# Experts of a mixture: the downs of two pairs in one run, the gate chain between the steps of the ups, the router in two row halves

## What is computed

```python
logits = flat @ router_w.T                        # flat: 512 x 64, layer-normed; 8 experts
probs = softmax(logits)
topk_probs, topk_idx = top_k(probs, 2)
topk_probs = topk_probs / (sum(topk_probs) + 1e-09)
gates = einsum('nk,nke->ne', topk_probs, onehot(topk_idx))
h1 = einsum('nc,ehc->neh', flat, w1)              # 682 hidden per expert
h3 = einsum('nc,ehc->neh', flat, w3)
y = einsum('neh,ech->nec', silu(h1) * h3, w2)
out = einsum('ne,nec->nc', gates, y)              # all experts are computed, the gate picks
```

## Time and profile before

| | us |
|---|---|
| median of three timed runs | 197.92 |
| lowest, highest | 196.71, 240.08 |
| profiled execution, its own time | 196.59 |
| span of the profiled execution | 194.8 |
| busy in it: TensorE, VectorE, ScalarE, GpSimd | 186.6, 151.4, 134.6, 97.9 |

### The profile page before, as it was taken

One profiled execution on the slowest core, in us unless ns is written; L12 is line 12 of the kernel. 1 busy time (PEld: TensorE's weight loads), 2 busy tenths in 40 slices (PEclk: granted clock), 3 DMA queues, 4 the chain that ended last, 5 costly groups with the idle time before them and its releaser, 6 DMA issues.

```text
span 194.8 us, 2708 instructions
## 1 busy us (share of the span) xinstructions
PE 186.6 (96%) x764; PEld 88.1 (45%) x766; DVE 151.4 (78%) x253; ACT 134.6 (69%) x298; POOL 97.9 (50%) x100
## 2 busy tenths in 40 slices
PE   7899999899999998999999999989999999999994
PEld 2334644354546453555455256836333324333332
DVE  6586899989999999999999955657776724888503
ACT  3729897999999999999999515355755614666200
POOL 6516667798999999999999700000000133100000
PEclk9999999999999999999999999799999999999999
DMA  5699372477768996799777993000000442000000
GB/s 155 140 227 191 112 257 106 179 219 255 235 214 240 294 308 220 251 309 303 244 265 214 192 204 47 3 0 0 2 3 3 128 114 59 24 0 3 0 0 27
DMA packets 23452, 28.00 MB, mean 144 GB/s; under 512 B 8153, under 2 KB 12734, under 8 KB 23438
## 3 DMA queue, kind: packets, MB, share of 16 engines
q1 hardware_dynamic: 23118, 27.67, 49.6%
q10 hardware_dynamic: 320, 0.16, 0.3%
HBM read 27.38 MB, written 0.44 MB: 143 GB/s over the span
## 4 chain that ended last, share of the span: by engine, by line
PE 67%; POOL 13%; issue 6%; DMA 5%; DVE 4%; ACT 3%; SPq 2%; POOLq 0%; DVEq 0%
PE ps L1246 17%; PE ps L1020 16%; POOL rings L474 12%; PE ps L1266 10%; PE ps L1027 4%; DMA cr<-bc_rows 3%; PE ps L1131 2%; DMA w_conv<-conv_w_dram 2%; PE ps L1006 2%; PE ps L985 1%; PE ps L945 1%; PE ps L1002 1%; ACT si L643 1%; PE ps L1046 1%; PE ps L1204 1%
## 5 line engine op out<-in xcount | busy, mean ns | idle before, releaser
L474 POOL TENSOR_TENSOR rings<-rings,cr 128x512 f32<-128x512 f32 x59 | 73.4, 1281 | 6.6 <-DVE rings L758 5.0
L758 DVE TENSOR_TENSOR_SCAN rings<-rings,ps 128x512 f32<-128x512 f32 x64 | 73.7, 1201 | 0.6
L566 ACT ACTIVATE rings<-delta,a_neg 128x510 f32<-128x510 f32 x64 | 46.7, 782 | 0.7 <-DVE rings L758 0.6
L643 ACT ACTIVATE si<-ps 128x512 f32<-128x512 f32 (+1 forms) x44 | 26.3, 597 | 23.0 <-PE ps L1246 23.0
L1246 PE MATMUL ps<-fd,wup 64*128 64x512 f32 (+1 forms) x136 | 40.3, 600 | 0.8 <-DVE fd L860 0.5
L547 ACT ACTIVATE scaled<-ps,b_tok 128x128 f32<-128x128 f32 x124 | 37.2, 443 | 0.0
L1020 PE MATMUL ps<-rings,ident 128*128 128x512 f32 x64 | 32.4, 599 | 1.0 <-POOL rings L474 0.9
L1020 PE MATMUL ps<-rings,flip 128*128 128x512 f32 x64 | 31.9, 601 | 0.5 <-POOL rings L474 0.2
L918 DVE TENSOR_TENSOR rings<-ps,si 128x512 f32<-128x512 f32 (+1 forms) x31 | 21.2, 690 | 13.5 <-ACT si L643 13.1
L496 POOL TENSOR_TENSOR fdg<-fd,gb 64x512 f32<-64x512 f32 x4 | 5.0, 1274 | 50.1 <-DMA gb<-g_rows 50.1
L1246 PEld LDWEIGHTS ps<-fd,wup 64*128 64x128 f32 (+1 forms) x136 | 15.7, 182 | 22.9 <-DVE rings L918 12.2
(11 more groups left out here) (222 smaller groups left out, 193.1 us busy)
## 6 DMA issues: line engine op xcount, KB each, us to landing
cr<-bc_rows SPq DMA_DIRECT2D x48, 256.0 KB, 4.0
br<-bc_rows SPq DMA_DIRECT2D x17, 256.0 KB, 4.4
cr<-c_rows SPq DMA_DIRECT2D x12, 256.0 KB, 3.7
wup<-w_up_dram SPq DMA_DIRECT2D x8, 341.0 KB, 6.3
wdn<-w_down_dram SPq DMA_DIRECT2D x4, 160.0 KB
wdn<-w_down_dram SPq DMA_DIRECT2D x4, 128.0 KB
gb<-g_rows SPq DMA_DIRECT2D x4, 128.0 KB, 4.6
delta<-g_rows SPq DMA_DIRECT2D x4, 128.0 KB, 3.6
```

Of the source, the lines that this page charges most:

```text
L474: nc.gpsimd.tensor_tensor(hc[:, q], hs[:, q], cr[:, row_slot(n)] if n >= ROWS_FROM else cs[:, q], ALU.mult).then_inc(weighted, 1)
L566: nc.scalar.activation(da[:, q, :, 1:L], delta[:, k, :].rearrange("p (b l) -> p b l", b=B)[:, :, 1:L], ACT.Exp, scale=a_neg[:, k * N + col ...
L643: nc.scalar.activation(si[0:rows, S % 2, :], ps[0:rows, BANK_H + 2 * (S % 3), :], ACT.Silu).then_inc(silu_ready, 1)
L758: nc.vector.tensor_tensor_scan(hs[:, q, :], da[:, q].rearrange("p b l -> p (b l)"), driven(q), 0.0, ALU.mult, ALU.add).then_inc(scanned, 1)
```

## The change

1. Downs in two runs: the downs of pairs 0 and 1 come together behind the ups of pair 1.
2. The gate chain moves from behind step 10 into pieces. ScalarE's table loads and exp stand behind the silu of step 7. VectorE's operations stand behind the products: five at step 7, two each at steps 8, 9, 10 and 11, seven at step 12. They are the same operations on the same data, each still waiting for the one before, and the last of a piece is waited for too. The transpose stays behind ups 13.
3. Router in row halves: the products of tokens 0 to 255 in rows 0 to 63 into bank 6, those of tokens 256 to 511 in rows 64 to 127 into bank 7, the halves in turn. The router's weights are loaded a second time for that, and `router_max` reads two banks.

```diff
-            sp.dma_start(w_rt[:], w_router).then_inc(qkv_in, 16)
+            for half in range(2):
+                sp.dma_start(w_rt[half * C:(half + 1) * C], w_router).then_inc(qkv_in, 16)
...
-                    if S == STEPS - 1:
+                    if S == 7:
                         nc.scalar.preload_act_table_set("exp_and_others")
                         act.wait_ge(lsub_ready, 1)
                         nc.scalar.activation(le[:], lo[:], ACT.Exp).then_inc(le_ready, 1)
                         nc.scalar.preload_act_table_set("silu_and_others")
...
             def router_max():
-                lps = ps[:, 7, 0:NT * E].rearrange("p (t e) -> p t e", t=NT)
+                lps = ps[:, 6:8, 0:NT // 2 * E].rearrange("p h (t e) -> p h t e", h=2, t=NT // 2)
+                largest = g1[:].rearrange("p (h t) -> p h t", h=2)
                 dve.wait_ge(lo_ready, NT)
-                chain(nc.vector.tensor_reduce(g1[:], lps, AX.X, ALU.max))
-                nc.vector.tensor_tensor(lo[:], lps, over(g1[:], E), ALU.subtract).then_inc(lsub_ready, 1)
+                chain(nc.vector.tensor_reduce(largest, lps, AX.X, ALU.max))
+                nc.vector.tensor_tensor(lo[:].rearrange("p (h t) e -> p h t e", h=2), lps,
+                                        largest.unsqueeze(3).broadcast_to([P, 2, NT // 2, E]), ALU.subtract).then_inc(lsub_ready, 1)
...
-            def gates():
-                softmax()
-                chain(nc.vector.tensor_reduce(m1[:], pb[:], AX.X, ALU.max))
...
+            def gate_step(S):
+                if S == 7:
+                    softmax()
+                    chain(nc.vector.tensor_reduce(m1[:], pb[:], AX.X, ALU.max))
+                    chain(nc.vector.tensor_tensor(key[:], pb[:], over(m1[:], E), ALU.is_equal))
+                elif S == 8:
+                    chain(nc.vector.tensor_tensor(key[:], key[:], ranks, ALU.mult))
+                    chain(nc.vector.tensor_reduce(g1[:], key[:], AX.X, ALU.max))
...
+                elif S == 12:
+                    chain(nc.vector.tensor_tensor(oh2[:], key[:], over(g1[:], E), ALU.is_equal))
+                    chain(nc.vector.tensor_tensor(oh1[:], oh1[:], oh2[:], ALU.add))
+                    chain(nc.vector.tensor_tensor(g2[:], m1[:], m2[:], ALU.add))
+                    chain(nc.vector.tensor_scalar(g2[:], g2[:], 1e-9, None, ALU.add))
+                    chain(nc.vector.reciprocal(g3[:], g2[:]))
+                    chain(nc.vector.tensor_tensor(pb[:], pb[:], over(g3[:], E), ALU.mult))
+                    nc.vector.tensor_tensor(gate[:], oh1[:], pb[:], ALU.mult).then_inc(gate_ready, 1)
+                    dve.wait_ge(gate_ready, 1)
...
                     if S == 2:
                         router_max()
-                    if S == STEPS - 1:
-                        gates()
+                    gate_step(S)
...
             def router():
-                for t in range(NT):
-                    nc.tensor.matmul(ps[:, 7, t * E:(t + 1) * E], fd[0:C, t * P:(t + 1) * P], w_rt[:], start=True,
-                                     stop=True).then_inc(lo_ready, 1)
+                for j in range(NT // 2):
+                    for half in range(2):
+                        t, rows = 2 * half + j, slice(half * C, (half + 1) * C)
+                        nc.tensor.matmul(ps[:, 6 + half, j * E:(j + 1) * E], fd[rows, t * P:(t + 1) * P], w_rt[rows], start=True,
+                                         stop=True).then_inc(lo_ready, 1)
...
-                if pair < PAIRS - FOLDED:
-                    for j in range(GROUPS):
-                        downs(pair, j)
+                if pair == PAIRS - FOLDED - 1:
+                    for done in range(PAIRS - FOLDED):
+                        for j in range(GROUPS):
+                            downs(done, j)
```

More of the change, by code:

```diff
@@ L94, in hybrid_kernel @@
         wqkv = sb("wqkv", [C + 1, 3, C])
-        w_rt = sb("w_rt", [C, E])
+        w_rt = sb("w_rt", [2 * C, E])
         wup = sb("wup", [2 * C, PAIRS, 2, HID])
@@ new lines, in gate_step @@
+            def gate_step(S):
[6 more added lines that the diff above has]
+                    chain(nc.vector.tensor_reduce(g1[:], key[:], AX.X, ALU.max))
+                elif S == 9:
+                    chain(nc.vector.tensor_tensor(oh1[:], key[:], over(g1[:], E), ALU.is_equal))
+                    chain(nc.vector.scalar_tensor_tensor(pb2[:], oh1[:], -4.0, pb[:], ALU.mult, ALU.add))
+                elif S == 10:
+                    chain(nc.vector.tensor_reduce(m2[:], pb2[:], AX.X, ALU.max))
+                    chain(nc.vector.tensor_tensor(key[:], pb2[:], over(m2[:], E), ALU.is_equal))
+                elif S == 11:
+                    chain(nc.vector.tensor_tensor(key[:], key[:], ranks, ALU.mult))
+                    chain(nc.vector.tensor_reduce(g1[:], key[:], AX.X, ALU.max))
+                elif S == 12:
[7 more added lines that the diff above has]
+                    dve.wait_ge(gate_ready, 1)
@@ L1118, in transpose_qk @@
                 pe.wait_ge(b_used, used_through(3 * N - 1))
-                pe.wait_ge(qkv_in, 32)
+                pe.wait_ge(qkv_in, 48)
                 for j in range(2):
```

## The result

The changed kernel takes **203.33 us** (median of four executions, 200.32 to 205.90), the kernel before 197.31 (median of four, 195.51 to 240.08). The change is slower, since the whole interval lies above 1; that it is so by more than 2% is not settled. The forecast was 202.1, or 1.0255 times the mean that it started from.

A forecast was written before the change was run, and what follows sets the result against it. The prediction took TensorE as the bound, its ups leading VectorE's products by only 0.13 us. Stalls of 5.66 less savings of 0.34 (router) and 0.27 (downs) gave +5.05 on 197.07: 202.1 us, range 199.0 to 204.8.

The forecast's parts named there:

- The lead of the ups: Ups lead VectorE's products by only 0.13 us, so silu 8's delay of 2.60 stalls TensorE 2.47 us before ups 11.
- The loads: Table loads and exp behind silu 7 keep ScalarE away 2.84 us; silu 8 starts at T + 3.46, 2.60 late.
- the drain: Rival: at the table switches, each load holds ScalarE as long again as it runs, 2.56 us more, 204.7; chance 0.03.
- The pieces: VectorE's chain operations at steps 8 to 12: 0.22 us each, products 1.05 apart, gate ready at T + 10.44.
- The sum: TensorE 5.66 us late at the gate's transpose, less savings of 0.34 and 0.27: +5.05 us; chance 0.48.
- the router's halves: Router's eight records, paired in row halves, take half of their 0.67 us: 0.34 us saved.
- one return from downs to ups: Running downs 0 and 1 together removes one change from downs back to ups: 0.27 us saved.
- the rival of the falling clock: TensorE's clock also falls around the two holes, 1.7 us more, 203.8 at most; chance 0.22.
- its sign of being right: Ups of step 14 follow those of step 7 by 12 us (11.9), confirming the sum's main term.
- Only the table loads cost: Rival: small operations overlap and the gate is ready when TensorE reaches the transpose; +2.0 us, 199.1; chance 0.14.
- Not slower: Rival: the ups' lead hides all the moved work, leaving only the savings, 196.5 us; chance 0.13.
- the cover decides: In the kernel before, the gate chain stands under the first run of downs, 5.30 us without need of ScalarE or VectorE.

The follow-up runs named there:

- filled: The changed kernel with matmuls nobody needs put into TensorE's two holes, ahead of ups 11 and of the gate's transpose; 202.60 us, ratio to before 1.0337.
- downs_only: The kernel before with only the order of the downs changed, the gate chain left whole behind step 10; ratio to before 1.0303.
- late_turn: The changed kernel with the gate's transpose and its copy on ScalarE behind ups 17 instead of ups 13; ratio to before 1.0217.
- no_tables: The changed kernel without the two table loads, a plain copy in place of the exp (gates not those of the reference); ratio to before 1.0192.
- after_three_runs: The changed kernel with the downs of pair 0 again behind pair 0, so three runs of downs; ratio to before 1.0046.
- no_tables_late: The changed kernel with a copy for the exp, no table loads, and the transpose behind ups 17; one execution, 197.76 us.
- under_downs: The kernel before with the router's halves and three VectorE operations (two gate multiplications, their addition) moved under runs of downs; ratio to before 0.9897.
- downs_filled: The kernel before with only the downs' order changed, plus eighteen spare matmuls in the hole ahead of the transpose; lowest time 199.82 us.

## Why the prediction was right, step by step

T is the start of silu 7, as in the prediction.

**The lead of the ups.** Right: a hole of 2.46 us ahead of ups 11 against 2.47, released by product 8.

**The loads.** Right: with T = 135.94, silu 8 starts at T + 3.45 (3.46). The load is 1.28 us and the next activation follows at once, here too; the drain that the Trainium skill (ScalarE: Activation LUTs, What ACT_TABLE_LOAD costs) adds to a switch is in none of these traces, and its rival is out.

**The pieces.** Right at full clock: in filled (T = 136.33) products 11 and 12 start at T + 7.28 and 8.32 (7.24 and 8.29), and the gate is done at T + 10.40 (10.44). In the changed kernel itself products 8 to 10 keep the forecast (T + 4.15, 5.19, 6.24; 4.09, 5.14, 6.19), and 12 comes at T + 9.22, because its ups ran at half clock. The spacing of 1.04 is 0.19 over an undisturbed step, which is the sum's own price; the sign that the prediction gave for being wrong, less than 0.2 a step, could not have told the two apart.

**The sum.** Right at full clock in its main term. Silu 14 of filled starts at 148.18 = T + 11.85, against T + 6.21 without a stall: 5.64 late, 5.66 forecast.

```profile
148.18 0.60 ACT L644 ACTIVATE si<-ps 128x512 f32<-128x512 f32 x1 [0.80 <-PE ps L1256]
```

Against before it is less, 4.65 and not 5.05, since three small terms were mis-sized:
- the router's halves give 0.43 over the stretch, 0.34 forecast;
- one return from downs to ups costs 0.37, 0.27 forecast (silus 10 and 11 of before start at 140.37 and 146.74; 6.37 less a step of 0.857 and 5.14 of downs; in the changed kernel the one return of pair 1 gives the same 0.37);
- the transpose was put at its 0.21 of the chain, but before it held the ups for 0.42 (silus 13 and 14 of before at 148.45 and 149.73, less 0.857), so 0.21 of the restart had been paid already.

```profile
146.74 0.60 ACT L643 ACTIVATE si<-ps 128x512 f32<-128x512 f32 x1 [2.92 <-PE ps L1246]
...
148.45 0.60 ACT L643 ACTIVATE si<-ps 128x512 f32<-128x512 f32 x1 [0.26 <-PE ps L1246]
...
149.73 0.60 ACT L643 ACTIVATE si<-ps 128x512 f32<-128x512 f32 x1 [0.53 <-PE ps L1246]
```

With these, 5.64 - 0.43 - 0.37 - 0.21 = 4.63.

**The clock.** Here the likeliest case was not what the profile shows: the rival of the falling clock came true, and its price was too low. It was put at 1.71 at most, from the one fall of the earlier trace rows; there were two falls, worth 2.48. So in the changed kernel itself silu 14 (149.67) comes 13.73 behind silu 7 and not the 11.9 that the prediction gave as its sign of being right, and the granted clock under 1 was among its signs of being wrong.

That the forecast of the time held is in part luck. In the stretch that the change touches, the profiles differ by 7.13 where 5.05 was forecast. The profile of before had its own fall at 121 us, and that of the changed kernel had none there; its ups start 1.43 earlier, which no run here shows to be the change's doing. So the difference of the two spans is +4.65 for the waits less the savings, +2.48 for the clock and -1.43 for the part ahead of the experts: 5.70. And the base, 197.07, was a mean of three executions that differ by 1.3 us among themselves.

What stays open is when the clock falls in such holes. It did in the profiles of the change and of downs_only. It did not in that of late_turn, which has the same first hole, nor in those of no_tables and after_three_runs with their holes of 2.35 and 2.21 ahead of the transpose, and one execution of the change at 200.32 us, with a mean granted clock of 0.991, was as quick as filled.

**The rivals.** "Only the table loads cost" is out: no_tables_late has no loads and no wait of the transpose and costs 2.06. "Not slower" is out by the first hole. That the cover decides, which the prediction said of the gate chain only (it stood under the downs), is shown by after_three_runs.

## What to carry to other kernels

Before moving work of a second engine, measure by how much the bound engine leads it: here three buffers gave 0.13 us, so that the work was all but free under the downs and was paid among the ups, whole or in pieces, but for the lead and the spare time of each step (2.46 of ScalarE's 2.84 us, 0.26 of each 0.68 us on VectorE). Look for the stretches in which the bound engine needs nobody, and put the others' extra work there; that gave 0.77 us of the 1% of under_downs, while an order that looked tidier lost 2.7%. An operation that waits in an in-order list should stand behind the step at which its data are ready, not the one at which they were ready in another order.

## What was not expected of the hardware

The clock of TensorE fell twice within 10 us, each time about the end of a hole of 2.0 to 2.5 us in dense work, and was granted in full in between, when TensorE was idle again (146 to 147 us: busy 0.00, clock 1.00). A hole of that size does not decide it alone: holes of 2.46, 2.35 and 2.21 us (late_turn, no_tables, after_three_runs), each alone or with one of under 1 us near it, left it at 1.00. With spare matmuls in the holes it stayed at 1.00 in the traces of filled and downs_filled, and they delayed nothing that the stretch shows. The Trainium skill (TensorE: Matmul & The Clock Gate, Why this matters for your kernels) advises to leave no long idle gap between bursts of matmuls; the change's trace agrees, with gaps of 2.5 and 2.0 us ahead of its two falls, and that of late_turn has a gap of 2.46 us and no fall.
